# A graph network in one kernel: the attentions' shift rows on 128 partitions, and x3 built as whole rows after the second attention

## What is computed

```python
def gat_conv(x, src, dst, W, a_src, a_dst, b):          # layer 0, three times, 4 heads of 192
    h = (x @ W).reshape(N, H, C)
    e = leaky_relu((h * a_src).sum(-1)[src] + (h * a_dst).sum(-1)[dst], 0.2)
    p = exp(e - segment_max(e, dst)[dst])
    alpha = p / (segment_sum(p, dst)[dst] + 1e-16)
    return segment_sum(alpha * h[src], dst) + b

# layer 2, 12 heads of 64 (_L2_gnn_ref)
alpha = w / maximum(segment_sum(w, dst)[dst], 1e-16)     # w as p above
agg = segment_sum(alpha[:, :, None] * ft[src], dst)
res = einsum('nhd,od->nho', hv, W_res)
out = relu((agg + res).reshape(n, H * DOUT))

x = _layernorm(x + _L2_gnn_ref(...))                     # x here is "x3" in the kernel
# layer 3: for each of 34 relations, mean over its edges @ W_rel[r], plus x @ W_root + b_rgcn; then a convolution
```

## Time and profile before

| | |
|---|---|
| median of 3 runs | 4101.87 us (4100.34 to 4104.19) |
| the profiled execution's own time | 4104.02 us |
| its span in the trace | 4102.4 us |
| mean granted TensorE clock | 0.968 |
| busy, share of the span | PE 92%, PEld 72%, DVE 48%, ACT 41%, POOL 38% |
| first attention, first to last exponential | from 623 to about 1202 us |
| second attention, first to last exponential | from 1765 to about 2206 us |
| root product | from 2221 to about 2307 us |

### The profile page before, as it was taken

One profiled execution on the slowest core, in us unless ns is written; L12 is line 12 of the kernel. 1 busy time (PEld: TensorE's weight loads), 2 busy tenths in 40 slices (PEclk: granted clock), 3 DMA queues, 4 the chain that ended last, 5 costly groups with the idle time before them and its releaser, 6 DMA issues.

```text
span 4102.4 us, 58268 instructions
## 1 busy us (share of the span) xinstructions
PE 3794.5 (92%) x18463; PEld 2939.7 (72%) x18473; DVE 1965.1 (48%) x2784; ACT 1702.3 (41%) x2902; POOL 1577.8 (38%) x1201
## 2 busy tenths in 40 slices
PE   8998769999988989679998999999999999989998
PEld 4554436777768889512223799999999999965588
DVE  7245787666633444699984333323223222013334
ACT  1114776666652321278995233333333333300021
POOL 3887885444420000001111244444444444357600
PEclk9999989999999999889999999999999999999999
DMA  4333112222223321221112355555555554369801
GB/s 142 101 105 74 37 22 63 65 71 74 59 79 106 100 69 55 100 81 58 51 45 94 105 183 181 180 184 184 184 182 182 180 184 138 111 229 303 266 17 63
DMA packets 204684, 483.10 MB, mean 118 GB/s; under 512 B 71582, under 2 KB 87989, under 8 KB 204566
## 3 DMA queue, kind: packets, MB, share of 16 engines
q1 hardware_dynamic: 115638, 201.96, 15.2%
q0 software_dynamic: 54368, 185.24, 14.6%
q10 hardware_dynamic: 34560, 94.45, 6.6%
HBM read 357.64 MB, written 123.55 MB: 117 GB/s over the span
## 4 chain that ended last, share of the span: by engine, by line
PE 43%; POOL 5%; DVE 5%; issue 3%; ACT 1%; DMA 0%; SPq 0%; DVEq 0%; ACTq 0%; POOLq 0%
PE ps L1913 29%; POOL work L1995 5%; PE ps L1245 3%; PE ps L1901 3%; PE ps L1587 3%; DVE work L1125 2%; PE ps L306 2%; PE ps L298 1%; DVE work L1153 1%; PE ps L1218 1%; ACT work L1308 1%; PE ps L324 0%; DMA work<-msg_d,work 0%; ACT ps L1299 0%; DVE mask L1762 0%
## 5 line engine op out<-in xcount | busy, mean ns | idle before, releaser
L1913 PE MATMUL ps<-wsplit,xsplit 128*128 x6840 | 1235.6, 337 | 1.3 <-POOL xsplit L1880 1.3
L1913 PEld LDWEIGHTS ps<-wsplit,xsplit 128*128 128x128 f32 x6840 | 1180.2, 188 | 1.5 <-issue 1.5
L1308 ACT ACTIVATE work<-ps,work 128x418 f32<-128x418 f32 x720 | 435.9, 607 | 239.7 <-PE ps L1218 238.8
L1255 PE MATMUL ps<-hbuf,work 128*128 128x193 f32 x2400 | 494.5, 345 | 13.2 <-DVE work L1170 13.1
L1880 POOL TENSOR_TENSOR xsplit<-ct,xsplit 128x768 fp32r<-128x768 f32 x190 | 368.8, 1941 | 298.5 <-ACTq L1945 298.4
L1153 DVE SCALAR_TENSOR_TENSOR work<-work,cnt 128x1250 f32<-128x1250 f32 x240 | 370.6, 1544 | 228.7 <-ACT work L1308 224.8
L1850 DVE CAST wsplit<-wplain 128x768 fp32r<-128x768 f32 x204 | 115.2, 565 | 760.3 <-PE ps L1913 742.3
L1950 ACT ACTIVATE ct<-ps,invs 128x768 f32<-128x768 f32 x190 | 171.5, 903 | 710.1 <-PE ps L1913 710.1
L1255 PEld LDWEIGHTS ps<-hbuf,work 128*128 128x128 f32 x2400 | 385.3, 191 | 83.4 <-issue 83.4
L1299 ACT ACTIVATE ps<-work,lr 128x418 f32<-128x418 f32 x720 | 418.5, 607 | 6.1 <-DMA work<-lrow_d 6.1
L1875 POOL DMA_INDIRECT ct<-x_d,relrec x190 | 198.5, 1045 | 516.9 <-PE ps L1901 497.0
(11 more groups left out here) (219 smaller groups left out, 4351.7 us busy)
## 6 DMA issues: line engine op xcount, KB each, us to landing
wplain<-in_L_gnn_W_rel SPq DMA_DIRECT2D x34, 2304.0 KB, 9.6
msg_d<-ct ACTq DMA_DIRECT2D x190, 384.0 KB, 2.6
work<-lrow_d SPq DMA_DIRECT2D x47, 625.0 KB, 3.8
feat_d<-work ACTq DMA_DIRECT2D x30, 386.0 KB, 3.4
hbuf<-feat_d SPq DMA_DIRECT2D x60, 193.0 KB, 2.5
gat_d<-work POOLq DMA_DIRECT2D x12, 960.0 KB, 5.2
xplain<-gat_d SPq DMA_DIRECT2D x30, 384.0 KB, 3.3
work<-xa_d SPq DMA_DIRECT2D x27, 384.0 KB, 3.2
```

The source lines that it names most:

```text
L1255: last = pe.matmul(ps[:, self.b0 + b, t * (C + 1):(t + 1) * (C + 1)], p[:, dt * P:(dt + 1) * P], self.feat(h, s), start=(s == 0 and t == 0 ...
L1308: act.activation(self.p[q % 3][:, c0:c1], ps[:, b, 0:c1 - c0], ACT.Exp, bias=self.l2[:, col:col + 1], scale=1.0 - SLOPE)\
L1913: last = pe.matmul(ps[:, 4 + 2 * (u % 2) + h, 0:HALF], x[:, u, c * P:(c + 1) * P], w[:, bass.ds(base + (c * D + h * HALF), HALF)], start=( ...
```

## The change

- `crow` and the ones become 128 partitions high. The rows are cleared once per attention; the DMA still writes partitions 0 to 2, the other 125 add zeros. This is in both attentions.
- `evict` of att2 writes its 64 columns straight into `z6`; `o`, `parts`, `pool_rows`, `columns_of_rows` and `stats6` go.
- `dve_root` now builds x3 tile by tile: `rows(j)` adds `res`, takes the relu and adds x2 over 768 columns, then runs the norm's usual sequence. From j = 2 on each is followed by the eviction `product(j - 2)`. Operands come as whole rows by `sp_parts`, two tiles deep: those of tiles 0 and 1 after the last maximum, those of tile j after tile j - 2 is ready. They share the queue with the bias and the first relation's weights.
- The six `split7` chunks go two each behind products 7, 8 and 9, and ScalarE takes the norm's root once per tile.

```diff
-                self.ones3 = cv(P, BF16, 3)
+                self.ones128 = cv(P, BF16)
...
-                self.crow = [cv(NP, BF16, 3) for _ in range(2)]
+                self.crow = [cv(NP, BF16) for _ in range(2)]
...
-                    sp.dma_start(self.crow[h % 2], shift_d[h]).then_inc(self.s_c_in[h % 2], 16)
+                    sp.dma_start(self.crow[h % 2][0:3, :], shift_d[h]).then_inc(self.s_c_in[h % 2], 16)
...
-                step(v.tensor_copy(self.ones3, ones[0:3, :]))
+                for row in self.crow:
+                    step.count(v.memset(row, 0.0))
+                step(v.tensor_copy(self.ones128, ones[:, :]))
...
-                        pe.matmul(ps[:, b, 0:c1 - c0], self.ones3, self.crow[h % 2][:, c0:c1], start=False, stop=True,
+                        pe.matmul(ps[:, b, 0:c1 - c0], self.ones128, self.crow[h % 2][:, c0:c1], start=False, stop=True,
...
-                    if self.narrow and q >= 2 * NT and q % (2 * NT) == late + 4:
-                        stats6(v, step, q // NT - 1)
                 evict(H - 1)
-                if self.narrow:
-                    v.wait_ge(s_cols6, H - 1)
-                    self.columns_of_rows(v, step, H - 1)
-                    stats6(v, step, H - 1)
...
+        def sp_parts(sp, j):
+
+
+            if j == 0:
+                sp.wait_ge(att2.s_max, att2.at["max"] + NT * att2.H)
+            if j >= 2:
+                sp.wait_ge(s_ready6, j - 1)
+            for k, dram in enumerate((res_d, x2_d)):
+                sp.dma_start(parts6[k][:, j % 2, :], dram[j * P:(j + 1) * P, :]).then_inc(s_parts6[j % 2], 16)
...
+            def rows(j):
                 z = z6[:, j, :]
-                v.tensor_scalar(z, z, mv6[:, j, 0:1], root6[:, j:j + 1], ALU.subtract, ALU.mult).then_inc(s_ready6, 1)
-            v.wait_ge(s_bias6, 16)
-            for j in range(NT):
+                v.wait_ge(s_parts6[j % 2], 32 * (j // 2 + 1))
+                step(v.tensor_tensor(z, z, parts6[0][:, j % 2, :], ALU.add))
+                step(v.scalar_tensor_tensor(z, z, 0.0, parts6[1][:, j % 2, :], ALU.max, ALU.add))
+                norm6.vector(v, step, z, j)
+                v.sem_inc(s_ready6, 1)
...
+            step.wait()
+            for j in range(NT):
+                rows(j)
+                if j >= 2:
+                    product(j - 2)
+            for j in range(NT - 2, NT):
+                product(j)
...
+            for j in range(2):
+                sp_parts(sp, j)
             sp.wait_ge(s_ready6, 1)
             sp.dma_start(brow6, a["L3_gnn_b_rgcn"].partition_broadcast(P)).then_inc(s_bias6, 16)
             sp.dma_start(w, rel[0]).then_inc(s_wrel, 16)
+            for j in range(2, NT):
+                sp_parts(sp, j)
...
             meet(g)
-            att2.pool_rows(g, step)
             pool_root(g, step)
```

More of the change, by code:

```diff
@@ L980, in __init__ @@
                 self.junk = cv(N)
-                self.o = [cv(NT * C) for _ in range(2)]
                 if self.narrow:
+                    self.head_out = lambda h, b: z6[:, self.tpb * b:self.tpb * (b + 1), h * C:(h + 1) * C]
                     self.flat = cv(NP)[0:C + 1, :]
@@ L985, in __init__ @@
                 else:
+                    self.o = [cv(NT * C).rearrange("p (t c) -> p t c", c=C) for _ in range(2)]
+                    self.head_out = lambda h, b: self.o[h % 2][:, self.tpb * b:self.tpb * (b + 1), :]
                     h5 = Carve(hbuf, NT * (D + 12))
@@ L1033, in unit_done @@
                     sp.wait_ge(self.s_agg, self.at["agg"] + (3 if self.narrow else 1) * (q + 1))
[L1035 to L1043, removed]
                 def shift(h):
@@ L1078, in sp @@
                             features(h + 2, 2 * k, 2 * k + 2)
-                    parts(h)
                     if h + 2 < H:
                         shift(h + 2)
[L1083 to L1096, removed]
             def pool(self, g, beside=lambda h: None):
@@ L1159, in evict @@
                         v.wait_ge(self.s_agg, self.at["agg"] + NT * (h + 1))
-                    if h >= 2 and self.narrow:
-                        v.wait_ge(s_cols6, h - 1)
-                    elif h >= 2:
+                    if h >= 2 and not self.narrow:
                         v.wait_ge(self.s_stored[h % 2], self.at["stored"] + 16 * (h // 2))
@@ L1778, in dve_root, with product @@
         def dve_root(v, step):
-            step.wait()
-            step.carry()
-            for j in range(NT):
-                step.count(v.bn_aggr(mv6[:, j, :], st6[:, j, :]))
-            step.wait()
-            step(v.tensor_scalar(root6, mv6[:, :, 1], EPS_LN, None, ALU.add))
-            v.sem_inc(norm6.var, NT)
-            v.wait_ge(norm6.root, norm6.b + NT)
-            step(v.reciprocal(root6, root6))
-            for j in range(NT):
-                z = z6[:, j, :]
-                v.tensor_scalar(z, z, mv6[:, j, 0:1], root6[:, j:j + 1], ALU.subtract, ALU.mult).then_inc(s_ready6, 1)
-            v.wait_ge(s_bias6, 16)
-            for j in range(NT):
+            def rows(j):
+                z = z6[:, j, :]
+                v.wait_ge(s_parts6[j % 2], 32 * (j // 2 + 1))
[3 more added lines that the diff above has]
+                v.sem_inc(s_ready6, 1)
+            def product(j):
+                if j == 0:
+                    v.wait_ge(s_bias6, 16)
                 v.wait_ge(W_ROOT.product, W_ROOT.b["product"] + j + 3)
                 v.tensor_tensor(halves(hbuf[:, j * D:(j + 1) * D]), W_ROOT.psum(j % 2), halves(brow6), ALU.add).then_inc(W_ROOT.emptied, 1)
-                c = j - 4
-                if c == 0:
+                if j == 7:
                     v.wait_ge(s_wrel, 16)
@@ L1801, in dve_root @@
                         v.wait_ge(s_st6[u], 16 * (NT // 2))
-                if c >= 0:
-                    split7(v, step, 0, c)
+                if j >= 7:
+                    for c in (2 * (j - 7), 2 * (j - 7) + 1):
+                        split7(v, step, 0, c)
+            step.wait()
[5 more added lines that the diff above has]
+                product(j)
         def act_root(act):
-            act.wait_ge(norm6.var, norm6.b + NT)
-            act.activation(root6, root6, ACT.Sqrt).then_inc(norm6.root, 1)
-            act.sem_inc(norm6.root, NT - 1)
+            for j in range(2):
+                norm6.scalar(act, j)
             for j in range(NT):
                 W_ROOT.take(act, j // 2, j % 2)
+                if j + 2 < NT:
+                    norm6.scalar(act, j + 2)
         def pool_root(g, step):
```

20 lines of the change are left out of this document (6 added, 14 removed).

## The result

Both kernels on the same chip: the changed one takes 3963.79 us (median of 4 runs, 3960.44 to 3965.84), the one before 4102.11 (4 runs, 4100.34 to 4104.19). The ratio is 0.9662, with an interval of 0.965 to 0.9674: 138 us faster. The forecast was 3974, with a range of 3955 to 4019.

What follows compares the result with a forecast made beforehand. TensorE bounds nearly everywhere, the second attention by three engines at once. First attention −102.5, second −29.5, root product +4.3 sum to −127.7: 4104.0 becomes 3976.3, and 3974 us with the median 2.1 lower; range 3955 to 4019.

Steps and rivals of the forecast that it cites:

- The cause of the first attention's loss: First attention: three-row shift matmuls lose 0.91 us a step by row count, not type; 128 rows should lose nothing.
- about 6: First attention, first head: two maxima per `weigh` hold the first five steps, so it saves about 6 us.
- Rival A: First attention: other engines hold the step at 4.2 us, 59 saved instead of 102, 4018 us in all; chance 0.12.
- rival C: Shift matmuls: a full-height weight load is exposed whole, some 0.10 us × 720 = 72 us, 4164 us; chance 0.03.
- So ScalarE stalls 1.4 + 1.0: Second attention: ScalarE stalls 2.4 us a head as `shifts` and `evict` delay `weigh`; a head takes 34.3, saving 2.5.
- there are only some 0.5 us to spare: Second attention: slack from the exponential's end through `weigh`, feature and shift matmul to ScalarE's next bank use, some 0.5 us.
- GpSimd's and the statistics' part: Second attention: about 3.2 and 1.0 us a head of VectorE's time go, leaving 30.5 to 31.
- +4.3: Root product: sum of its terms +0.4, +2.4 and +1.5, a cost of 4.3 us (0 to 11).
- 12.5: Root product: the third tile's rows, queued behind bias and weights, take about 12.5 us and land at about 2230.5.
- +2.4: Root product: TensorE gets the third tile late, costing 2.4 us (0 to 8).
- The last splits: End of the root product: VectorE splits two chunks behind product 9, costing 1.5 us (0 to 3).
- Rival D: Root product: loads run one behind another, 3 us per tile on eight tiles, +24, 3998 us; chance 0.05.

Runs made afterwards that it cites:

- e1: The kernel before with nothing but the 128-row shift, x3 still built by columns; 4005.48 us, ratio 0.9706 to the kernel before.
- e4: The changed kernel with 64 rows in `crow` and the ones instead of 128; 4121.68 us, ratio 0.9993 to the kernel before.
- e5: The changed kernel with 65 rows in `crow` and the ones instead of 128; 3967.87 us, ratio 0.9674 to the kernel before.
- e2: The changed kernel with shift rows and ones on 3 partitions again; 4119.72 us, ratio 0.9988 to the kernel before.
- e8: The changed kernel itself, unaltered, run again in the second batch; 3961.53 us, ratio 0.966 to the kernel before.

## Why the prediction was right, and where it was off

**The cause of the first attention's loss: right.** The rows and not the type, by the earlier trace rows; e1 shows it alone, and e4 against e5 with everything else equal. The step is 3.8 us; a head was forecast at 39.24 and measured at 39.42. The first head won 7.35 us instead of "about 6", but only half of that is the rows'. In both kernels it begins at the lower clock, and in the trace of the kernel before this lasts some 8 us longer than in that of the changed one. The same window of both, before and after, columns as in the earlier trace rows:

```profile
631.00:638.50 7.50, 7.50 (x21) 5.39 (x21) 6.29 (x9) 3.36 (x6) 5.07 (x3) 0.50 0.11 26
...
631.00:638.50 7.50, 7.50 (x47) 7.11 (x46) 7.09 (x10) 6.46 (x13) 5.98 (x6) 1.00 0.03 3
```

e2, with three rows too, has the full clock by 634 us, 8 us into its attention, and its first ten steps take 44.37 us, against 48.06 before and 40.70 in the changed kernel. So some 3.7 us are the rows' and 3.7 are the clock of one execution; "about 6" was too much, and from e2's 581.9 us the whole stage moves −101.9, nearer to the forecast's −102.5 than the −105.6 of the two traces. Double maxima do hold the head once the rows are tall, at the forecast 4.40 us a step. Clearing the two rows took 1.2 us instead of 0.8, and hid: the first shift matmul starts 0.3 us earlier than before. Rival A (other engines hold the step at 4.2) and rival C (an exposed full-height load) did not come about.

**The second attention: mechanism right, stalls mis-sized.** "So ScalarE stalls 1.4 + 1.0, and a head takes 31.9 + 2.4 = 34.3" is the term that was off. The floor was good (32.41 measured, less 0.28 of waits, is 32.13); the stall was a ninth of what was charged. `weigh` is late as forecast: in the changed kernel's trace the one behind `shifts` starts 1.81 us after the exponential that it waits for has ended, the one behind `evict` 1.08 (0.5 and 0.8 a step later, most others 0.03). What was wrong is the next step, "there are only some 0.5 us to spare". TensorE waits for both (1.76 and 1.08 us, the 16 waits above), but ScalarE waits only behind `evict`, 0.28 us once a head: the lateness of 1.08 loses 0.28, so some 0.8 are to spare. Behind `shifts` it loses nothing, for there it has the three copies of the last head's sums to do, 1.2 us (L1289, from 1799.10 to 1802.00 between its exponentials), which the forecast had counted as load and not as work that fills the wait. `weigh` itself behaved as forecast, 1.42 to 1.46 us in this attention (up to 1.53 in the first). By evictions the nine heads won 39.2 us where 22 were forecast; the first head won 1.2 (forecast 1), the last two 6.0 (6.5). All 17 us of the error lie in this one term. GpSimd's and the statistics' part was counted as time of VectorE, and that was right: it is busy 247.70 us in eight heads, 31.0 a head, where 30.5 to 31 were forecast. That each half would be worth less alone (16.7 and 14.2 us of 46.4) was not said.

**The root product: +8.6 instead of +4.3.** The first product came +0.4 later, as forecast. The rows of the third tile were forecast to land 12.8 us behind tile 0's readiness and landed 15.2 behind it: the queue's "12.5" was measured as 13.8, and it only counts from the issue, 1.4 us later, since four DMA instructions go out one after another. So the term "+2.4" is 5.0: the third tile's transposes start 13.86 us behind the first product's start, 8.82 before. The gap itself is 4.02 us, where the forecast named 2 to 3 as its sign. The clock behind the gap was not priced at all: the transposes held TensorE 0.46 us longer (1.12 instead of 0.66) and the second product took 1.28 more. The last splits cost 1.40 (forecast 1.5). 0.4 + 5.0 + 0.5 + 1.3 + 1.4 is the whole 8.6. Rival D, gaps at later tiles, did not come about.

**The total** of 3974 against 3963.8 is closer than its parts. Between the two traces the forecast was 13.6 us off: −17 in the second attention, −3 in the first (nearly all of it the clock of one execution), +4 in the root product, +4 in the later stages and −1.5 ahead of and between the attentions. That the two errors of +4 make up for part of the others is luck. The medians are 10 us off, since the profiled execution before was 1.9 us above its median and the one after 1.1 below.

## What to carry to other kernels

When a matmul on few rows stands among full-height ones, compare the starts of its neighbours, not its own duration; if they are apart by more than the streaming, try to pad the contraction past 64 rows with zeros, which cost nothing here (shown for bfloat16 matmuls of 416 columns among full-height float32 ones, with 3 and 64 rows against 65 and 128). Where three engines are within 10% of each other, halves of a change say little about the whole: list each engine's busy time per period after each edit, and the next bound is the largest. And when work is moved to the far side of a stage boundary, put what the first consumer needs ahead of bulk loads in the same queue: 384 + 384 KB behind 2.7 MB cost some 6 to 7 us here, a gap of 4 and the slower clock around it.

## What was not expected of the hardware

- The threshold in rows is sharp and lies between 64 and 65: 48.40 us a head against 39.53. That it is a matter of half the array's height fits the number; why the hardware does so no run here shows. No height between 3 and 64 was tried.
- The shorter load cost on both its sides: a shift matmul held TensorE 0.10 us longer, the float32 instruction behind it 0.10 longer than its fellows, and the one ahead as much again, 0.30 in all, 0.91 a step. Two loads that do not overlap (0.09 and 0.19 us long) stand in that place; how the three tenths divide among them is not shown.
- Behind 4.02 us without work, in the middle of a run of products, TensorE's granted clock was 0.70 over five us, between its two levels of 1.2 and 2.4 GHz, and the product there took 9.19 us instead of 7.91. With the transposes ahead of it the price behind the gap was 1.74 us; it was 1.75 in e2, e4 and e8 (gaps of 3.5 to 3.9 us) and 1.37 in e5 (4.4).
